# Layer 0 of a four-layer model in one kernel: a batch's end spread over 40 steps, its inverse roots taken on GpSimd

## The chip, the cores and the metric

The kernel runs on one core of a Trainium2 chip, as one program. The metric is the time of one execution on the device in microseconds (us). A difference is read from several runs of both kernels on the same chip.

## The reference

The whole program is four layers, each "normalise, then x + attention(xn) + ffn(xn)", on x of 8 batches x 512 positions x 128 features. The change touches layer 0 alone, whose attention has relative positions (16 heads of 8 features) and ends in a normalisation of its own, and whose feed-forward part is a product with the signs of a weight:

```python
def _layernorm(x, axis=-1, eps=1e-05):
    m = jnp.mean(x, axis=axis, keepdims=True)
    v = jnp.var(x, axis=axis, keepdims=True)
    return (x - m) / jnp.sqrt(v + eps)
...
    scores = scores + (c2p + p2c) / scale          # [8, 16, 512, 512]
    probs = jax.nn.softmax(scores, axis=-1)
    ctx = jnp.einsum('bhqk,bhkd->bhqd', probs, v)
    ctx = jnp.transpose(ctx, (0, 2, 1, 3)).reshape(B, S, H)
    out = ctx @ Wo + bo + hidden_states
    mu = jnp.mean(out, axis=-1, keepdims=True)
    var = jnp.mean(jnp.square(out - mu), axis=-1, keepdims=True)
    out = (out - mu) * jax.lax.rsqrt(var + LN_EPS) * ln_scale + ln_bias
...
    b_weight = jnp.sign(weight)
    return jnp.einsum('bsi,oi->bso', x, b_weight)  # L0 feed-forward
...
    x = x + _L0_attn_ref(xn, ...) + _L0_ffn_ref(xn, L0_ffn_weight)
```

## The kernel before

Layer 0 is one software pipeline over 512 blocks of scores. A block is 128 query positions by 512 key positions of one head; four blocks are a head, 16 heads a batch, so 64 blocks a batch and 8 batches. Each engine runs its own Python loop over the same step number `u`, with `b, r = divmod(u, 64)`: `r` is the step within a batch. The order of the work on each engine is that of its loop, and semaphores tie the engines together.

In step `u` TensorE computes the scores of block `u` (`scores`) and transposes the probabilities of block `u-4` (`p_tr`). VectorE adds the band of relative positions into block `u-1` (`add`, a 192 or 256 column tensor_tensor on PSUM) and takes its negated row maximum (`most`, line 193, once a block). ScalarE takes the exponential of block `u-2` (`exp`, line 167) and copies the transposed probabilities of block `u-5` (`p_out`, line 171). Three PSUM banks hold scores, so the scores of block `v` wait for the exponential of block `v-3`.

Once a head, each in two halves, there are also: a 512 column copy-and-add of the position products by VectorE (`g_out`, at steps with `ib` 1 and 3), a 512 column correction by GpSimd that `g_out` needs (`corr`, at `ib` 0 and 2), and the own band by GpSimd (`own_band`, at `ib` 2: one product of 192 columns and one of 768, which the `add` of the next head needs). GpSimd's order in a head is the second correction, the own band, the first correction of the following head. The band comes back from DRAM by a transfer of SyncE (`write`, `read`). Probabilities times v (`pv`) run on TensorE once per four heads, as four groups of matmuls in steps 5, 7, 9 and 11 of every 16.

All rarer work goes through one PSUM bank, in an order written out by hand: `AHEAD` gives the steps at which the next batch's q, k, far columns, g0 and v are computed, `HEADS` and `ENDS` those at which a finished batch is brought to its end. `small(u)` turns the tables into the list `order`, and each use waits until the one before it has been emptied. The end of batch b-1 runs inside batch b:

- `heads`, `ct`, `mo`: context heads gathered, transposed, multiplied with Wo (plus xn); VectorE adds the bias into `T1` (`tail` 0)
- `sw`: xn times the sign weights; VectorE adds it into X, and takes the mean and variance of `T1` (`tail` 1)
- `root`: ScalarE's square root of the four variances of each partition (line 167)
- `norm`: VectorE's `newton`, that is the reciprocal of the root and one Newton step, and four tensor_scalars of 128 columns that normalise `T1` (`tail` 2)
- `sum`: GpSimd's `tail`, three 512 column tensor_tensors (scale, bias, and the sum into X)
- `last`: VectorE's statistics of X for the next layer's norm (`tail` 3)

The last entry of `ENDS` is for the end of the last batch, which runs in 28 extra steps after the last block, with nothing beside it. After layer 0 every engine waits for all of it (`after_l0`), and layer 1 begins with a norm whose square roots are ScalarE's.

Of the kernel before, what the change touches and what calls it, by code (L numbers as in the profile page):

```python
# [9 lines left out]
ALU = mybir.AluOpType  # L10
# [132 lines left out]
def flat(ap):  # L143
    return ap.rearrange("p a b -> p (a b)")
# [21 lines left out]
def act(ac, out, in_, func, bias=0.0, scale=1.0, accum=None):  # L166
    return ac.e.activation(out, in_, func, bias=bias, scale=scale, accum_out=accum)  # L167
# [12 lines left out]
def tt(en, out, in0, in1, op):  # L180
    return en.e.tensor_tensor(out, in0, in1, op)  # L181
# [24 lines left out]
def newton(dv, y, v, tmp):  # L206

    dv.step(dv.e.reciprocal(y, tmp))
    dv.settle()
    dv.step(tt(dv, tmp, y, y, ALU.mult))  # L210
    dv.settle()
    dv.step(tt(dv, tmp, tmp, v, ALU.mult))
    dv.settle()
    dv.step(ts(dv, tmp, tmp, -0.5, 1.5, ALU.mult, ALU.add))
    dv.settle()
    return tt(dv, y, y, tmp, ALU.mult)


def program(nc, a, out):
    ctx = ExitStack()  # L220
    with ctx:
# [102 lines left out]
        def tr(pe, out, in_):  # L324
# [44 lines left out]
        CTT = flat(T1)  # L369
        nst4 = A0.take(4, 6)  # L370
        lst, lmv, ly, lv, ltmp = A0.take(4, 6), A0.take(4, 2), A0.take(4), A0.take(4), A0.take(4)
        NT0 = dict(st=flat(PB[0].rearrange("p (a b) -> p a b", b=1))[:, 0:192].rearrange("p (a b) -> p a b", b=6),
                   mv=PB[1][:, 0:64].rearrange("p (a b) -> p a b", b=2),
                   y=PB[2][:, 0:32], v=PB[2][:, 64:96], tmp=PB[2][:, 128:160])
# [2 lines left out]

        dv_init, po_init, op_init = sem("dv_init"), sem("po_init"), sem("op_init")
        PT_0, GG_0 = 1, 4
        PGO_0, VA_0 = 1, 3  # L380
        sgn, set_mm, set_dv, set_ac, sel_ok, pg_w, pg_r = (sem("set_" + k) for k in ("sgn", "mm", "dv", "ac", "sel", "pgw", "pgr"))
        s_mm, s_ad, s_mx, s_ex, t_mm, to_a = (sem("l0_" + k) for k in ("s_mm", "s_ad", "s_mx", "s_ex", "t_mm", "to_a"))
        g_mm, g_o, p_cr, p_w = (sem("l0_" + k) for k in ("g_mm", "g_o", "p_cr", "p_w"))
# [12 lines left out]

        AHEAD = {"q": 1, "k": 3, "far": 13, "g0": 15, "v": 35}
        XF_OUT = {2: "q", 4: "k", 14: "far", 16: "g0"}  # L400
        SPLIT_AT = 5
        HEADS = (33, 47, 62)
        ENDS = [{"heads": 17, "ct": 19, "mo": 29, "sw": 31, "root": 34, "norm": 36, "sum": 38, "last": 48}] * NB
        ENDS += [{"heads": 14, "ct": 16, "mo": 18, "sw": 19, "root": 21, "norm": 22, "sum": 23, "last": 25}]

        def small(u):

# [183 lines left out]
        def l0_dv(dv):  # L591
# [100 lines left out]
            def tail(b, k):  # L692
                ps, xs = quarters(PS[:, B_M, :]), slice(b * 4, b * 4 + 4)
                if k == 0:
                    dv.wait_ge(m_mm, number["mo", b, 0] + 1)
                    dv.wait_ge(ld_end, 3 * 16)
                    tt(dv, T1, ps, bc(bot.unsqueeze(1), [128, 4, 128]), ALU.add).then_inc(m_dv, 1)
                elif k == 1:
                    dv.wait_ge(m_mm, number["sw", b, 0] + 1)
                    tt(dv, X[:, xs, :], ps, X[:, xs, :], ALU.add).then_inc(m_dv, 1)  # L700
                    dv.wait_ge(*emptied[number["mo", b, 0]])
                    dv.settle()
                    stats(dv, lmv, lst, T1)
                    dv.settle()
                    ts(dv, lv, lmv[:, :, 1], 1e-7, None, ALU.add).then_inc(tn_v, 1)
                elif k == 2:
                    dv.wait_ge(tn_v, b + 1)
                    dv.wait_ge(tn_q, b + 1)
                    dv.step(newton(dv, ly, lv, ltmp))
                    dv.settle()  # L710
                    for q in range(4):
                        ins = ts(dv, T1[:, q, :], T1[:, q, :], lmv[:, q, 0:1], ly[:, q:q + 1], ALU.subtract, ALU.mult)
                    ins.then_inc(tn_n, 1)
                else:
                    dv.wait_ge(t1_ok, b + 1)
                    stats(dv, NMV[:, xs, :], nst4, X[:, xs, :])
# [5 lines left out]
            for u in range(STEPS0 + 1):  # L722
                n, ib = divmod(u, 4)
                b, r = divmod(u, 64)
                if 0 <= u - 1 < 4 * NBH:
                    add(u - 1)
                if ib in (1, 3) and n + 4 < NBH:
                    g_out(n + 4, ib // 2)
                if 0 <= u - 1 < 4 * NBH:
                    most(u - 1)  # L730
                if b >= 1:
                    at = ENDS[b]
                    if r == at["heads"] + 1:
                        heads_out(b - 1, 3)
                    if r == at["mo"] + 1:
                        tail(b - 1, 0)
                    if r == at["sw"] + 1:
                        tail(b - 1, 1)
                    if r == at["norm"]:
                        tail(b - 1, 2)  # L740
                if b + 1 < NB and r == AHEAD["v"] + 1:
                    v_out(b + 1)
                if b < NB and r - 1 in HEADS:
                    heads_out(b, HEADS.index(r - 1))
                if b >= 1 and r == ENDS[b]["last"]:
                    tail(b - 1, 3)


        def l0_ac(ac):
# [80 lines left out]
            for u in range(STEPS0 + 1):  # L830
                n, ib = divmod(u, 4)
                b, r = divmod(u, 64)
                if 0 <= u - 2 < 4 * NBH:
                    exp(u - 2)
                if 0 <= u - 5 < 4 * NBH:
                    p_out(u - 5)
                if b + 1 < NB:
                    if r in XF_OUT:
                        xf_out(XF_OUT[r], b + 1)
                    k, late = divmod(r - SPLIT_AT, 3)  # L840
                    if 0 <= k < 6 and late == 0:
                        split_ac(b + 1, k // 2, k % 2)
                G, k = divmod(u - 28, 16)
                if k == 0 and 0 <= G < 4 * NB:
                    os_out(G)
                if b >= 1:
                    if r == ENDS[b]["ct"] + 1:
                        ct_out(b - 1)
                    if r == ENDS[b]["root"]:
                        ac.wait_ge(tn_v, b)  # L850
                        act(ac, ltmp, lv, ACT.Sqrt).then_inc(tn_q, 1)


        def l0_po(po):
            po.e.memset(PGO, 0.0).then_inc(po_init, 1)
            for k in range(2):
                po.e.memset(VA[k], 1.0).then_inc(po_init, 1)

            def split(b, k, half):

# [55 lines left out]
            for u in range(STEPS0 + 1):  # L916
                n, ib = divmod(u, 4)
                b, r = divmod(u, 64)
                if ib == 0 and n + 4 < NBH:
                    corr(n + 4, 1)  # L920
                if ib == 2 and n + 1 < NBH:
                    own_band(n + 1)
                if ib == 2 and n + 5 < NBH:
                    corr(n + 5, 0)
                k, late = divmod(r - SPLIT_AT - 2, 3)
                if b + 1 < NB and 0 <= k < 6 and late == 0:
                    split(b + 1, k // 2, k % 2)
                if b >= 1 and r == ENDS[b]["sum"]:
                    tail(b - 1)

# [1642 lines left out]
```

## Time and profile before

| | |
|---|---|
| median of 3 runs | 2280.51 us (2279.85 to 2285.18) |
| profiled execution, its own time | 2277.15 us |
| its span, first to last instruction | 2275.3 us |
| mean granted clock of TensorE | 0.96 |
| busy: TensorE, VectorE, ScalarE, GpSimd | 85%, 78%, 63%, 54% of the span |
| layer 0's blocks, first to last row maximum | 75.4 to 921.3 us |

The profile is one execution recorded by the hardware. A row of a table of stretches gives the stretch, its length, the busy time (and instructions) of PE, PEld, DVE, ACT and POOL in it, the granted clock, the share of the DMA engines and GB/s. "Busy" is the time in which an engine worked on an instruction; issue, branches and waits are not in it. VectorE starts an instruction up to 0.1 us before the one ahead has ended, so what an instruction costs in a row of them is the distance between starts. A row says in brackets how long the engine had sat idle before it, and what ended that. Most helpers record all their calls under one line: 181 is any tensor_tensor, 176 and 177 a tensor_scalar, 157 a matmul. So an instruction is known by its engine, its operation, its shape and its tiles; AR is one large tile that holds most of layer 0's buffers.

### The profile page before, as it was taken

What the parts mean: (1) busy time and instruction counts of PE and PEld (TensorE: products, weight loads), DVE (VectorE), ACT (ScalarE), POOL (GpSimd) and SP (SyncE); (2) the same over time, 40 slices, a digit from 0 to 9 for tenths busy, and PEclk for the clock granted to TensorE, in tenths of its full rate; (3) what the DMA queues carried; (4) which work ended last, traced back from release to release, by engine and by line L of the source; (5) the groups of instructions that cost most, each with busy time, mean ns of one, the idle gap of its engine ahead of it and who ended that gap; (6) DMA issues with size and microseconds to landing.
All of it is one profiled execution on the core that took longest, in us unless ns stands there. A gap on an engine that the chain in (4) does not pass through costs nothing.

```text
span 2275.3 us, 38965 instructions
## 1 busy us (share of the span) xinstructions
PE 1944.4 (85%) x13526; PEld 1473.7 (65%) x13526; DVE 1763.7 (78%) x4099; ACT 1430.5 (63%) x2795; POOL 1223.2 (54%) x1028
## 2 busy tenths in 40 slices
PE   3799898888989898587996999999998468788898
PEld 2566565666666666464683878777876345566797
DVE  7688888888888888457187888888887699873586
ACT  2578777777878777344235666666665257765575
POOL 3777677777777775148053445444543466426400
PEclk9999999999999999789997999999999689999999
DMA  3988788888878786201000000000001000003000
GB/s 105 306 304 303 249 294 274 288 268 278 284 271 281 278 300 227 85 1 35 3 6 1 1 1 1 1 1 1 1 1 31 0 0 1 1 1 98 24 2 38
DMA packets 73877, 264.15 MB, mean 116 GB/s; under 512 B 12273, under 2 KB 32241, under 8 KB 73169
## 3 DMA queue, kind: packets, MB, share of 16 engines
q1 hardware_dynamic: 72304, 254.31, 33.2%
q10 hardware_dynamic: 1376, 7.34, 0.8%
q8 instruction: 109, 1.79, 0.3%
q14 instruction: 88, 0.71, 0.1%
HBM read 140.30 MB, written 121.31 MB: 115 GB/s over the span
## 4 chain that ended last, share of the span: by engine, by line
PE 38%; DVE 8%; ACT 6%; POOL 2%; issue 2%; DMA 0%; POOLq 0%; ACTq 0%; DVEq 0%; SPq 0%
PE PS L157 10%; PE PS L161 7%; PE PS L163 7%; PE PS L162 7%; PE PS L326 7%; ACT AR L167 3%; ACT L167 2%; DVE AR L181 1%; DVE DR L181 1%; DVE PT L181 1%; ACT AR L171 1%; ACT PT L171 1%; DVE AR L185 1%; DVE AR L200 1%; DVE AR L193 1%
## 5 line engine op out<-in xcount | busy, mean ns | idle before, releaser
L167 ACT ACTIVATE AR<-PS,AR 128x512 f32<-128x512 f32 x1008 | 686.6, 688 | 286.8 <-DVE AR L193 178.8
L193 DVE TENSOR_REDUCE AR<-PS 128x1 f32<-128x512 f32 x896 | 616.4, 688 | 119.3 <-PE PS L163 100.5
L326 PE MATMUL PS<-ident,AR 128*128 128x128 f32 x3816 | 584.6, 277 | 86.1 <-ACT AR L171 38.6
L157 PE MATMUL PS<-AR 128*9 128x512 f32 (+8 forms) x4190 | 503.5, 360 | 93.0 <-DVE AR L181 32.9
L326 PEld LDWEIGHTS PS<-ident,AR 128*128 128x128 f32 x3816 | 435.0, 142 | 200.6 <-issue 71.2
L181 POOL TENSOR_TENSOR AR<-AR 128x512 f32<-128x512 f32 (+6 forms) x310 | 380.6, 1244 | 226.9 <-DVE AR L181 97.0
L157 PEld LDWEIGHTS PS<-AR 128*9 128x9 f32 (+5 forms) x4190 | 288.8, 133 | 298.4 <-DVE AR L181 130.1
L171 ACT ACTIVATE AR<-PS 128x512 f32<-128x512 f32 (+3 forms) x612 | 356.4, 587 | 91.8 <-PE PS L326 47.7
L176 POOL TENSOR_SCALAR AR<-AR 128x512 f32<-128x512 f32 x144 | 245.4, 1704 | 293.2 <-DVE AR L1596 219.4
L171 ACT ACTIVATE PT<-PS 128x512 fp32r<-128x512 f32 x320 | 191.5, 599 | 208.3 <-PE PS L326 171.5
L181 DVE TENSOR_TENSOR PS<-PS,AR 128x192 f32<-128x192 f32 (+1 forms) x512 | 201.7, 394 | 118.0 <-PE PS L534 112.0
L181 DVE TENSOR_TENSOR AR<-PS,AR 128x512 f32<-128x512 f32 (+3 forms) x321 | 210.0, 655 | 40.8 <-PE PS L157 36.2
L181 POOL TENSOR_TENSOR AR<-XN,AR 128x192 f32<-128x192 f32 (+1 forms) x170 | 201.5, 1206 | 60.9 <-DMA XN<-scr 42.9
L181 DVE TENSOR_TENSOR PT<-PS,PT 128x512 fp32r<-128x512 f32 x320 | 217.7, 680 | 5.0 <-ACT PT L171 5.0
L181 POOL TENSOR_TENSOR AR<-AR,XN 128x512 f32<-128x512 f32 x144 | 154.3, 1074 | 104.4 <-DVE AR L181 74.8
L534 PE MATMUL PS<-AR 128*128 128x320 bf16 (+3 forms) x1024 | 197.3, 275 | 0.0
L531 PE MATMUL PS<-ident,XN 128*128 128x128 f32 x680 | 131.1, 275 | 0.0
L161 PE MATMUL PS<-MH,XNr 128*128 128x512 f32 x256 | 123.5, 483 | 5.2 <-ACT AR L167 2.8
L176 DVE TENSOR_SCALAR AR<-AR 128x512 f32<-128x512 f32 (+6 forms) x229 | 113.9, 501 | 1.3
L534 PEld LDWEIGHTS PS<-AR 128*128 128x128 bf16 x1024 | 101.1, 99 | 6.2
L163 PE MATMUL PS<-MH,XNr 128*128 128x512 f32 x256 | 102.1, 399 | 0.0
L161 PE MATMUL PS<-PT,VW 128*128 128x512 f32 x256 | 101.5, 396 | 0.0
(157 smaller groups left out, 3001.9 us busy)
## 6 DMA issues: line engine op xcount, KB each, us to landing
scr<-AR SPq DMA_DIRECT2D x128, 800.0 KB, 4.3
XN<-scr SPq DMA_DIRECT2D x85, 768.0 KB, 6.6
AR<-scr SPq DMA_DIRECT2D x43, 768.0 KB, 6.5
AR<-qsc SPq DMA_DIRECT2D x96, 192.0 KB
qsc<-AR SPq DMA_DIRECT2D x96, 128.0 KB, 3.4
AR<-in_wgu SPq DMA_DIRECT2D x16, 256.0 KB, 3.2
X<-in_x ACTq DMA_DIRECT2D x1, 2048.0 KB, 8.5
AR<-in_wi ACTq DMA_DIRECT2D x1, 2048.0 KB, 8.2
```

The lines of the kernel that those rows point to most:

```text
L157: return pe.e.matmul(out, lhsT, rhs, start=start, stop=stop)
L161: pe.e.matmul(out, l[0], r[0], start=start, stop=False)
L162: pe.e.matmul(out, l[1], r[0], start=False, stop=False)
L163: return pe.e.matmul(out, l[0], r[1], start=False, stop=stop)
L167: return ac.e.activation(out, in_, func, bias=bias, scale=scale, accum_out=accum)
L171: return ac.e.activation(out, in_, ACT.Copy, bias=0.0, scale=1.0)
L176: return en.e.tensor_scalar(out, in0, s1, None, op0)
L181: return en.e.tensor_tensor(out, in0, in1, op)
L193: return dv.e.tensor_reduce(out, in_, AX.X, ALU.max, negate=True)
L326: return pe.e.transpose(out, in_, ident[0:k, 0:k])
L531: pe.e.matmul(out, lhsT, rhs, start=start, stop=start, is_transpose=True, skip_group_check=True)
L534: return pe.e.matmul(out, lhsT, rhs, start=False, stop=stop, skip_group_check=True)
```

## The change

The tables of steps are rewritten, the square root on ScalarE becomes a power of -0.5 on GpSimd (four columns, with a constant tile `minus_half`), and the Newton step is written with three instructions in place of five. The X add has a `tail` part of its own. The statistics' `tail` 1 runs at step 32 of VectorE's loop as before, `norm` goes from 36 to 41, the sign-weight matmuls from 31 to 45 and their add from 32 to 46, GpSimd's `tail` from 38 to 47, the last statistics from 48 to 57, and the next batch's v from 35 to 51.

```diff
+def newton3(dv, y, v, tmp):
+
+    dv.step(stt(dv, y, tmp, -0.5, tmp, ALU.mult, ALU.mult))
+    dv.settle()
+    dv.step(tt(dv, y, y, v, ALU.mult))
+    dv.settle()
+    return stt(dv, y, y, 1.5, tmp, ALU.add, ALU.mult)
...
-        AHEAD = {"q": 1, "k": 3, "far": 13, "g0": 15, "v": 35}
+        AHEAD = {"q": 1, "k": 3, "far": 13, "g0": 15, "v": 51}
...
-        ENDS = [{"heads": 17, "ct": 19, "mo": 29, "sw": 31, "root": 34, "norm": 36, "sum": 38, "last": 48}] * NB
-        ENDS += [{"heads": 14, "ct": 16, "mo": 18, "sw": 19, "root": 21, "norm": 22, "sum": 23, "last": 25}]
+        ENDS = [{"heads": 17, "ct": 19, "mo": 29, "stats": 32, "root": 34, "norm": 41, "sw": 45, "sum": 47, "last": 57}] * NB
+        ENDS += [{"heads": 14, "ct": 16, "mo": 18, "stats": 19, "root": 19, "norm": 20, "sw": 19, "sum": 21, "last": 22}]
...
                 elif k == 1:
-                    dv.wait_ge(m_mm, number["sw", b, 0] + 1)
-                    tt(dv, X[:, xs, :], ps, X[:, xs, :], ALU.add).then_inc(m_dv, 1)
                     dv.wait_ge(*emptied[number["mo", b, 0]])
...
-                    dv.step(newton(dv, ly, lv, ltmp))
+                    dv.step(newton3(dv, ly, lv, ltmp))
...
+                elif k == 3:
+                    dv.wait_ge(m_mm, number["sw", b, 0] + 1)
+                    tt(dv, X[:, xs, :], ps, X[:, xs, :], ALU.add).then_inc(m_dv, 1)
...
-                    if r == at["sw"] + 1:
+                    if r == at["stats"]:
                         tail(b - 1, 1)
                     if r == at["norm"]:
                         tail(b - 1, 2)
+                    if r == at["sw"] + 1:
+                        tail(b - 1, 3)
...
-                    if r == ENDS[b]["root"]:
-                        ac.wait_ge(tn_v, b)
-                        act(ac, ltmp, lv, ACT.Sqrt).then_inc(tn_q, 1)
...
+            po.e.memset(minus_half, -0.5).then_inc(po_init, 1)
...
+                if b >= 1 and r == ENDS[b]["root"]:
+                    po.wait_ge(po_init, HALF_0)
+                    po.wait_ge(tn_v, b)
+                    tt(po, ltmp, lv, minus_half, ALU.pow).then_inc(tn_q, 1)
```

## Rows read from the trace of the kernel before

**Rows 1.** The page: busy time and share of each engine.

```profile
PE 1944.4 (85%) x13526; PEld 1473.7 (65%) x13526; DVE 1763.7 (78%) x4099; ACT 1430.5 (63%) x2795; POOL 1223.2 (54%) x1028
```

**Rows 2.** Table of stretches: blocks 28 to 59 of the first and third batch.

```profile
120.89:168.58 47.69, 44.81 (x403) 31.87 (x403) 42.21 (x87) 37.31 (x67) 35.87 (x33) 1.00 0.89 298
327.98:384.85 56.87, 47.81 (x426) 34.25 (x426) 49.37 (x114) 40.18 (x70) 40.26 (x37) 1.00 0.75 251
```

**Rows 3.** Stretches: batch 0's blocks 30, 35, 47; the third's 30, 31, 35, 40-43, 47, 48-51.

```profile
123.48:124.47 0.99, 0.99 (x14) 0.89 (x12) 0.95 (x4) 0.64 (x2) 0.91 (x2) 1.00 0.18 71
...
130.72:132.79 2.07, 2.07 (x23) 1.29 (x20) 2.07 (x4) 1.58 (x3) 1.19 (x2) 1.00 1.00 337
...
148.64:150.60 1.96, 1.56 (x14) 1.06 (x11) 1.93 (x6) 1.96 (x4) 1.96 (x3) 1.00 1.06 336
...
332.36:334.04 1.68, 1.68 (x20) 1.58 (x19) 1.05 (x3) 0.78 (x2) 1.05 (x1) 1.00 0.49 202
334.04:337.51 3.47, 2.19 (x19) 1.61 (x16) 3.40 (x14) 1.57 (x3) 2.37 (x2) 1.00 0.99 328
...
342.27:347.88 5.61, 3.13 (x24) 1.72 (x24) 5.44 (x13) 3.27 (x6) 2.36 (x2) 1.00 1.01 299
...
354.02:360.16 6.14, 6.14 (x56) 3.70 (x50) 5.17 (x12) 4.57 (x9) 6.14 (x7) 1.00 0.68 241
...
363.74:366.87 3.13, 1.65 (x14) 1.06 (x11) 3.06 (x13) 1.96 (x4) 2.54 (x3) 1.00 1.00 313
366.87:371.92 5.05, 3.98 (x37) 3.30 (x38) 4.98 (x11) 3.98 (x8) 3.01 (x4) 1.00 0.76 271
```

**Rows 4.** Timeline, third batch, step 32: VectorE and GpSimd.

```profile
336.55 0.17 DVE L176 TENSOR_SCALAR AR<-AR 128x4 f32<-128x4 f32 x1
...
334.15 2.37 POOL L181 TENSOR_TENSOR AR<-XN,AR 128x192 f32<-128x192 f32 x2 [0.58 <-DVE PS L181]
```

**Rows 5.** Timeline of a later layer: VectorE's small tensor_scalar beside GpSimd.

```profile
1834.06 1.43 DVE L176 TENSOR_SCALAR AR<-AR 128x4 f32<-128x4 f32 x1
...
1831.14 4.33 POOL L181 TENSOR_TENSOR AR<-AR 128x1024 f32<-128x1024 f32 x2
```

**Rows 6.** Timeline, third batch, step 36: VectorE's Newton and normalisation, GpSimd's own band.

```profile
343.08 1.88 DVE L181 TENSOR_TENSOR AR<-AR 128x4 f32<-128x4 f32 x2
...
345.39 1.11 DVE L177 TENSOR_SCALAR AR<-AR 128x128 f32<-128x128 f32 x4
...
342.38 2.36 POOL L181 TENSOR_TENSOR AR<-AR 128x192 f32<-128x192 f32 x2 [0.58 <-DVE PS L181]
```

**Rows 7.** Timeline, GpSimd and VectorE: second batch's steps 56 and 57, batch 0's 40 and 41.

```profile
269.62 2.38 POOL L181 TENSOR_TENSOR AR<-XN,AR 128x192 f32<-128x192 f32 x2
271.95 1.05 POOL L181 TENSOR_TENSOR AR<-AR 128x512 f32<-128x512 f32 x1
...
272.04 0.42 DVE L181 TENSOR_TENSOR PS<-PS,AR 128x256 f32<-128x256 f32 x1
...
138.93 2.37 POOL L181 TENSOR_TENSOR AR<-XN,AR 128x192 f32<-128x192 f32 x2 [2.30 <-DMA XN<-scr]
```

**Rows 8.** Timeline of ScalarE, third batch, around the root.

```profile
339.42 1.28 ACT L167 ACT_TABLE_LOAD   x1
...
342.23 0.69 ACT L167 ACTIVATE AR<-PS,AR 128x512 f32<-128x512 f32 x1
```

**Rows 9.** Timeline of GpSimd, third batch, step 46's correction.

```profile
360.68 1.05 POOL L181 TENSOR_TENSOR AR<-AR,XN 128x512 f32<-128x512 f32 x1
```

**Rows 10.** Timeline, the last batch's end: VectorE; ScalarE, its DMA issue and first root.

```profile
936.27 0.69 DVE L181 TENSOR_TENSOR X<-PS,X 128x512 f32<-128x512 f32 x1 [1.25 <-PE PS L157]
...
939.05 0.18 DVE L208 RECIPROCAL AR<-AR 128x4 f32<-128x4 f32 x1 [0.69 <-ACT AR L167]
...
945.81 0.46 ACTq L1314 DMA_DIRECT2D AR<-in_wo  x1
...
946.85 0.31 ACT L167 ACTIVATE AR<-AR 128x8 f32<-128x8 f32 x2 [8.25 <-DVE AR L176]
```

More of the change, by code:

```diff
@@ L371, in program @@
         lst, lmv, ly, lv, ltmp = A0.take(4, 6), A0.take(4, 2), A0.take(4), A0.take(4), A0.take(4)
+        minus_half = A0.take(4)
         NT0 = dict(st=flat(PB[0].rearrange("p (a b) -> p a b", b=1))[:, 0:192].rearrange("p (a b) -> p a b", b=6),
@@ L379, in program @@
         PT_0, GG_0 = 1, 4
-        PGO_0, VA_0 = 1, 3
+        PGO_0, VA_0, HALF_0 = 1, 3, 4
         sgn, set_mm, set_dv, set_ac, sel_ok, pg_w, pg_r = (sem("set_" + k) for k in ("sgn", "mm", "dv", "ac", "sel", "pgw", "pgr"))
@@ L745, in l0_dv @@
                 if b >= 1 and r == ENDS[b]["last"]:
-                    tail(b - 1, 3)
+                    tail(b - 1, 4)
         def l0_ac(ac):
```

## The prediction

> **What bounds the kernel now.** I read the page first: VectorE is busy 78% and TensorE 85% of the span [rows 1]; a mean over four layers says little, and the diff touches only layer 0. So I cut layer 0 by its own beat. VectorE takes one row maximum (line 193) for each 128x512 block of scores, 64 a batch. "Block k" is the stretch from the start of maximum k of a batch to that of the next; VectorE's extra work of loop step r lies in block r-1. The table of stretches then compares the same blocks of different batches [rows 2]. Batch 0 ends no other batch: its blocks 28 to 59 take 47.69 us. The third batch takes 56.87 us for them, and the second batch's end is what it has more. All 9.2 us between them is that end.
>
> Finer stretches show where [rows 3]. Block 30, before which the sign-weight matmuls now run, takes 1.68 against batch 0's 0.99. Block 31 (line 181's add into X, the statistics, the variance) takes 3.47, VectorE busy 3.40. Block 35 (Newton, four normalisations, the v copy) takes 5.61 against 2.07, VectorE busy 5.44: nothing but VectorE decides there, and TensorE is busy only 3.13. Blocks 40 to 43 take 6.14 with TensorE busy all of it and VectorE only 5.17, since the four probability-times-v groups run there; the like four blocks without them (48 to 51) take 5.05, VectorE busy 4.98. So there are two regimes. VectorE sets 12 to 19, 28 to 35, 44 to 51 and 60 to 3; TensorE sets the others, and there VectorE has 6.14 - 5.05 = 1.09 us of slack in four blocks. A VectorE instruction costs its issue interval in the first kind and nothing, up to the slack, in the second.
>
> **The change, term by term**, for one of the seven batch ends inside the loop, against the third batch.
>
> 1. *Sign-weight matmuls leave step 31.* They had waited there for the T1 add. Block 30 falls to batch 0's 0.99 [rows 3]: **-0.69**. They come back at step 45, in a region that VectorE sets, behind the same kind of queue: I take the same 0.69 there, **+0.69** (nothing at best, twice that at worst).
>
> 2. *The add into X leaves step 32.* It takes 0.60 from its start to the next one's, so block 31 would be 2.87. But the variance's tensor_scalar now comes 0.6 sooner after the maximum. Now it starts at 336.55, at the very end of GpSimd's two own-band products (334.15 to 336.52) [rows 4]. Elsewhere the same 4-column instruction beside a GpSimd tensor_tensor takes 1.43 us and not 0.17, and ends with GpSimd's [rows 5]. I expect it to be held to the same moment: -0.60 + 0.56 = **-0.04** (-0.6 if it is not held). The add returns at step 46 in a VectorE region: **+0.60**.
>
> 3. *Newton and the normalisations leave step 36.* Block 35 falls from 5.61 to batch 0's 2.07 [rows 3]: **-3.54**. What goes: five Newton steps, of which the first tensor_tensor is held for some 1.7 us by GpSimd's 128x768 product (1.88 for the pair of it and an ordinary one), and four tensor_scalars [rows 6]. The v matmuls and v copy leave steps 35 and 36 too, but come back at 51 and 52, the same place of the 16-step pattern: I count zero for both together.
>
> 4. *Newton at step 41.* Three instructions at some 0.20 from start to start, as the small ones of [rows 6]: 0.60. Four normalisations, 1.03 (the 1.11 of their row less the 0.08 by which the next instruction starts early). And a hold: all three Newton instructions read two SBUF operands. Where block 40's neighbour sixteen steps on is undisturbed, GpSimd ends its own-band pair at 272.0 and starts the next 1.05 us correction at 271.95; VectorE is free at 272.04 [rows 7]. So it meets the correction, not the long own-band product: 271.95 + 1.05 - 272.07 = 0.93 us held. The ends are 0 (the instruction slips in first) and some 2.6: in batch 0 the own band, late from its read, runs from 138.93 to 141.30 while VectorE is free at 139.52 [rows 7], 1.75 us, and the correction behind it could hold the second instruction for another 0.85. 0.93 is the row nearest. From 0.60 + 1.03 + 0.93 = 2.56 the slack of blocks 41 and 43 is taken, 1.09: **+1.47**.
>
>    The Trainium skill ("SBUF — State Buffer", Who interferes with whom) says that the pair of ports which VectorE shares with GpSimd is an exclusive lock, taken by a VectorE instruction with two SBUF inputs against a GpSimd one that reads SBUF. By that rule step 41 is no safe place either; the held row above agrees, with 1.88 us for two 4-column instructions, and the 0.93 above is what it comes to. Without such a rule the term would be 0.54.
>
> 5. *X's statistics go from step 48 to 57.* Out of a VectorE region: block 47 takes 3.13 against batch 0's 1.96, **-1.17**. In block 56, where TensorE sets again, the same 1.17 meets the same slack of 1.09: **+0.08**.
>
> 6. *The root moves from ScalarE to GpSimd.* ScalarE loses two table loads of 1.28 us and a 0.20 us root [rows 8]. I count **zero**: during them VectorE and TensorE go on, and the exponential behind them starts at 342.23 just when VectorE enters its 5.6 us block, in which it catches up. If that cover were gone, they would cost 2.8. The Trainium skill ("ScalarE: Activation LUTs", What ACT_TABLE_LOAD costs) gives 2.66 us for a switch with its drain, 5.3 for both; by it alone the removal would be the larger part of the change. The trace shows 2.81 from the first load's start to the next exponential's, and no other engine waiting for it.
>    GpSimd gets the power after the correction of step 34, where it then sits idle some 2 us for VectorE. No row shows a power. Below it is bounded by what four columns take on VectorE, 0.17 us [rows 6], above by GpSimd's own-band pair, 2.36 us for 960 columns; I take 1.0, since four columns are few and a power is not one operation. Behind it queue the correction of step 36, the own band (2.36) and a correction, due at step 41. From that correction's end to step 41 pass some 11.5 us in batch 0, 4.5 of them GpSimd's own work, so some 7 us are free and all of the range costs nothing.
>
> 7. *GpSimd's three 512-column products move from step 38 to 47*, 3.9 us. Behind them wait the correction for step 51 and the own band for step 53. In the third batch the correction ahead of them starts at 360.68 [rows 9]: 360.68 + 1.05 + 3.9 + 1.05 = 366.7 for the next, which VectorE uses at 368.87, and 2.36 more, 369.0, for the own band, used after 371.9. Both are some 2 us ahead: **zero**.
>
> Sum: -0.69 + 0.69 - 0.04 + 0.60 - 3.54 + 1.47 - 1.17 + 0.08 = **-2.60 us** a batch end, times seven **-18.2 us**.
>
> *The last batch's end* is a bare chain [rows 10]. Statistics no longer wait for the sign matmuls, 1.25, and the add, 0.60: -1.85. The root's hop is 0.69, its own 0.20 in it; by GpSimd I take 0.25 + 1.0, so +0.56. Two Newton steps fewer, -0.40. But ScalarE's last table load, hidden now in a wait, must come before layer 1's first root, behind the barrier and two DMA issues: they end at 946.27, plus 1.28 is 947.55 and not 946.85, +0.70. Together **-1.0**.
>
> The profiled execution took 2277.15 (span 2275.3), 0.15% under the median of 2280.51. It goes to 2277.15 - 19.2 = 2258.0; as a median of runs, 2280.51 - 19.2 = **2261.3 us**, 0.8% faster.
>
> **Rivals.**
> *A, the hold comes in full and the slack isn't there.* Own-band reads land late without the old stall, as in batch 0, so Newton is held 2.6 us, and TensorE gives back nothing: +1.67 + 1.09 leaves +0.16 a batch, nothing in all: 2280.6, no change. For it: the DMA engines are busier where there is no stall (0.89 of batch 0's stretch against 0.75 [rows 2]). Against: at the undisturbed place the own band starts 0.2 us after the add that it waits for, its read long there [rows 7]. Chance 0.13.
> *B, no hold at all.* Newton meets no GpSimd instruction, and the variance neither: -0.93 - 0.56 a batch, -10.4: 2250.9. Chance 0.15.
> *C, GpSimd becomes late (slower).* The power stands in a queue that is busy 4.5 of every 5.05 to 6.1 us (two corrections and an own band). It costs nothing up to some 7 us and a microsecond each beyond. To lose 0.3% it must use up 19.2 + 6.8 in seven batches, 3.7 us each: a power of about 11 us, 2.7 us a column, where a column of the own band costs 2.5 ns (2.36 us over 960). At 12 us it gives back 5 a batch: 2261.3 + 35 = 2296. Against: nothing on GpSimd in this trace is near it; for: a power is not an ordinary operation, and no row prices it. Chance 0.06.
> *D, the table loads were on the path*: 2.8 more a batch, 2241.7. Against: VectorE is busy 5.44 of 5.61 behind them. Chance 0.06.
> The forecast itself 0.60, its own range 2254 to 2269 (the ends of terms 1, 2 and 4, a microsecond a batch either way).
>
> **How the numbers follow.** 0.3%, 6.8 us, is about what a measurement tells from no change. Faster: 0.60 + 0.15 + 0.06 and a fifth of A, 0.84; same 0.10; slower 0.06. Eight in ten: from B, with its neighbours' microsecond, 2248, to halfway to A, 2272.
>
> **What would show it.** Block 35 near 1.5 to 2.1; block 30 near 1.0; block 31 unchanged near 3.4, its variance held; a Newton instruction of 0.9 to 1.1 us in block 40, block 40 about 3.6 and the blocks 41 to 43 shorter by about 1; block 47 near 2; block 56 longer by 1.2 with 57 to 59 shorter; no table loads between exponentials; the power well under 2 us. I am wrong if the own band or a correction of steps 41 to 55 makes VectorE wait for GpSimd, or if the blocks that TensorE sets grow by what VectorE was given.

## The result, and the profile after

The changed kernel takes 2260.2 us (median of 4 runs, 2258.81 to 2263.45) beside 2280.18 us for the kernel before on the same chip (4 runs, 2279.63 to 2285.18): a ratio of 0.991, 95% interval 0.9892 to 0.9927. The forecast was 2261.3. Its profiled execution took 2258.81, span 2257.0, 18.3 less than the span before. The page's line of busy times hardly differs from [rows 1]; means over the program say nothing here either.

```profile
PE 1943.3 (86%) x13526; PEld 1476.4 (65%) x13526; DVE 1760.9 (78%) x4083; ACT 1409.8 (62%) x2773; POOL 1230.6 (55%) x1037
```

The table of stretches of the kernel after, for the blocks of [rows 2] and [rows 3]. Columns: start:end and length; busy time (and instructions) of PE, PEld, VectorE, ScalarE, GpSimd; granted clock, DMA share, GB/s. First blocks 28 to 59 of batch 0 and of the third batch, then the third batch's 30, 31, 35, 36 to 39, 40, 41 to 43, 47 and 56 to 59.

```profile
120.44:167.51 47.07, 44.82 (x403) 31.85 (x403) 42.24 (x87) 37.14 (x67) 36.01 (x34) 1.00 0.90 302
323.14:376.30 53.16, 46.95 (x421) 33.84 (x421) 48.60 (x112) 36.88 (x66) 41.16 (x38) 1.00 0.78 267
327.52:328.51 0.99, 0.76 (x9) 0.79 (x10) 0.96 (x3) 0.27 (x1) 0.82 (x1) 1.00 0.13 52
328.51:331.86 3.35, 2.04 (x17) 1.45 (x15) 3.28 (x13) 1.97 (x4) 2.54 (x3) 1.00 1.04 353
...
335.92:337.39 1.47, 0.94 (x9) 0.65 (x8) 1.47 (x3) 1.47 (x4) 1.47 (x3) 1.00 1.11 374
337.39:344.13 6.74, 6.74 (x66) 4.15 (x67) 5.21 (x12) 5.10 (x10) 4.91 (x5) 1.00 1.00 302
344.13:347.64 3.51, 3.51 (x37) 2.02 (x36) 3.37 (x11) 1.18 (x2) 1.56 (x2) 1.00 0.75 295
347.64:351.63 3.99, 2.89 (x31) 2.26 (x23) 3.96 (x8) 2.91 (x6) 2.29 (x3) 1.00 0.44 154
...
356.26:358.22 1.96, 1.76 (x15) 1.18 (x12) 1.92 (x5) 1.89 (x4) 1.88 (x3) 1.00 1.05 359
...
370.07:376.30 6.23, 5.79 (x53) 3.48 (x53) 6.13 (x19) 4.09 (x8) 4.26 (x5) 1.00 0.67 247
```

What a batch's end costs over batch 0 went from 9.2 us to 53.16 - 47.07 = 6.1. Block 35, 5.61 before, is now 1.47. Block 40 is the new long one, 3.51. In blocks 40 to 43 VectorE is busy 3.37 + 3.96 = 7.33 of the 7.50 us and TensorE only 6.40: with Newton in it, VectorE sets this stretch too.

The timeline of VectorE and GpSimd in the third batch, kernel after: the variance of step 32, the power of step 34 (the second of the pair at 332.02, 1.03 us; the first is a correction, 1.01), Newton and the normalisations of step 41.

```profile
330.43 0.65 DVE L176 TENSOR_SCALAR AR<-AR 128x4 f32<-128x4 f32 x1
...
344.73 0.99 DVE L185 SCALAR_TENSOR_TENSOR AR<-AR 128x4 f32<-128x4 f32 x1
345.75 0.16 DVE L181 TENSOR_TENSOR AR<-AR 128x4 f32<-128x4 f32 x1
...
346.15 1.12 DVE L177 TENSOR_SCALAR AR<-AR 128x128 f32<-128x128 f32 x4
...
329.24 1.81 POOL L181 TENSOR_TENSOR AR<-XN,AR 128x768 f32<-128x768 f32 x1
332.02 2.04 POOL L181 TENSOR_TENSOR AR<-AR 128x512 f32<-128x512 f32 x2 [0.96 <-DVE AR L181]
...
342.31 2.38 POOL L181 TENSOR_TENSOR AR<-XN,AR 128x192 f32<-128x192 f32 x2
344.64 1.06 POOL L181 TENSOR_TENSOR AR<-AR 128x512 f32<-128x512 f32 x1
```

The rows show two holds, that is, VectorE instructions drawn out until a GpSimd one ends. The variance's 4-column instruction takes 0.65 us and not 0.17, and ends at 331.08, GpSimd's 128x768 product at 331.05. Newton's first instruction starts at 344.73, just behind the start of a correction that runs to 345.70, and ends at 345.72; the next two, alone, take 0.16. The root is no visible part of this: VectorE doesn't wait for the power anywhere inside a batch.

### The profile page after: what moved, and what is told of

It reads as the page before. It is cut to its first block, busy times and chain, and to the rows that moved or that the text cites. A ratio compares the mean times of both kernels' runs of the same rounds, so it can differ in the third digit from the quotient of the medians.

```text
span 2257.0 us, 38937 instructions
## 1 busy us (share of the span) xinstructions
PE 1943.3 (86%) x13526; PEld 1476.4 (65%) x13526; DVE 1760.9 (78%) x4083; ACT 1409.8 (62%) x2773; POOL 1230.6 (55%) x1037
## 4 chain that ended last, share of the span: by engine, by line
PE 38%; DVE 9%; ACT 5%; POOL 2%; issue 2%; DMA 0%; POOLq 0%; ACTq 0%; DVEq 0%; SPq 0%
PE PS L157 9%; PE PS L161 7%; PE PS L163 7%; PE PS L162 7%; PE PS L335 7%; ACT AR L167 2%; DVE AR L181 2%; ACT L167 1%; DVE PT L181 1%; DVE DR L181 1%; ACT AR L171 1%; DVE AR L185 1%; DVE AR L193 1%; DVE AR L200 1%; DVE XN L177 1%
## 5 line engine op out<-in xcount | busy, mean ns | idle before, releaser
L181 POOL TENSOR_TENSOR AR<-AR 128x512 f32<-128x512 f32 (+6 forms) x318 | 388.3, 1238 | 248.7 <-DVE AR L181 89.0
```

## Experiments

Each run is set beside runs of the kernel before that were measured together with it (medians 2278.04, 2280.37 and 2278.43). Undoing one part of the change is measured from the kernel after, whose ratio is 0.991. The diffs show the lines or words that differ, without what stands around them.

**1. The new steps with ScalarE's root.** Only the steps are changed; the power is gone, root and table loads are back on ScalarE, and Newton has its five instructions.

```diff
-    tt(po, ltmp, lv, minus_half, ALU.pow).then_inc(tn_q, 1)
+    act(ac, ltmp, lv, ACT.Sqrt).then_inc(tn_q, 1)
-                    dv.step(newton3(dv, ly, lv, ltmp))
+                    dv.step(newton(dv, ly, lv, ltmp))
```

> The changed kernel's steps, but the root is ScalarE's square root again and Newton has its five instructions. Two ideas of what the power on GpSimd is worth. (a) The table loads are hidden wherever they stand: only two more Newton instructions, 0.2 us each, in seven batches, some 3 us: 2263 us, block 34 to 35 at 1.0 and 1.5 us as in the changed kernel. (b) They were hidden before only by VectorE's long block 35 behind them; at the new steps that cover is gone and most of the 2.8 us of two loads and a root shows in each of seven batches: 2260 + 3 + up to 19.6, so 2275 to 2282, with VectorE idle in blocks 34 to 36 waiting for TensorE, which waits for ScalarE. The prediction's words were: if that cover were gone, they would cost 2.8.

Measured: 2279.28 us (10 runs), ratio 0.9997, 0.9986 to 1.0008. The whole gain is gone. Timeline of the third batch of this kernel, ScalarE, then VectorE and TensorE:

```profile
336.37 1.28 ACT L167 ACT_TABLE_LOAD   x1
...
339.19 0.69 ACT L167 ACTIVATE AR<-PS,AR 128x512 f32<-128x512 f32 x1
...
342.42 0.37 DVE L181 TENSOR_TENSOR PS<-PS,AR 128x192 f32<-128x192 f32 x1 [3.19 <-PE PS L544]
...
340.41 1.12 PE L335 MATMUL PS<-ident,AR 128*128 128x128 f32 x4 [2.33 <-ACT AR L171]
```

And its table of stretches: blocks 35 and 36 to 39 of the third batch, then block 35 of the fourth:

```profile
338.54:343.29 4.75, 2.88 (x14) 2.68 (x15) 1.56 (x3) 4.04 (x7) 2.52 (x3) 0.60 1.00 343
343.29:351.30 8.01, 8.01 (x64) 4.33 (x65) 5.26 (x11) 4.58 (x8) 3.87 (x4) 0.81 0.54 141
448.63:452.51 3.88, 2.00 (x16) 1.60 (x16) 1.56 (x4) 3.87 (x7) 2.58 (x3) 1.00 0.99 326
```

VectorE is idle for 3.19 us in block 35, behind TensorE, which has itself waited 2.33 us for a ScalarE copy that came behind the loads. In this batch there is a second cost: the granted clock is 0.60 over block 35, and the four transposes at 340.41 take 1.12 us, against 0.66 for the like four at 374.26 of the kernel after. Blocks 34 to 39 take 4.57 us more than in the kernel after, which is more than the 2.8 us from the first load to the next exponential. In the fourth batch TensorE waits the same 2.33 us and the clock stays at 1.00: block 35 takes 3.88 and not 4.75, and the whole batch is 2.15 us longer than that of the kernel after, the two more Newton instructions (0.19) among them. The other six batches have the low clock. Over all seven this trace is 22.7 us longer, 3.2 a batch. So with the move the table loads lie on the path, at about 2 us in the batch where the clock stays up and more where it falls.

**2. The old steps with GpSimd's power** and Newton's three instructions: the other half of the change.

```diff
-    act(ac, ltmp, lv, ACT.Sqrt).then_inc(tn_q, 1)
+    tt(po, ltmp, lv, minus_half, ALU.pow).then_inc(tn_q, 1)
-                    dv.step(newton(dv, ly, lv, ltmp))
+                    dv.step(newton3(dv, ly, lv, ltmp))
```

> The kernel before with its own steps, but the root is GpSimd's power and Newton has three instructions. (a) As the prediction has it, the loads cost nothing at the old steps: the gain is two Newton instructions, 0.4 us in seven batches, 3 us, and the last batch's end is shorter by 0.4 and longer by the power's hop and the late table load, about +0.9: 2278 us, block 35 near 5.2 us. (b) If the loads were on the path at the old steps, 2.8 a batch more: 2258 us. The hold in block 35 stays in both, near 1.7 us.

Measured: 2281.07 us (10 runs), ratio 1.0004, 0.9994 to 1.0015. No change. Block 35 falls only from 5.61 to 5.23, the two Newton instructions fewer. Timeline of this kernel's third batch, VectorE, then TensorE:

```profile
338.96 1.70 DVE L181 TENSOR_TENSOR AR<-AR 128x4 f32<-128x4 f32 x1
...
343.53 0.40 PE L157 MATMUL PS<-AR 128*128 128x128 bf16 x4 [2.85 <-DVE AR L181]
...
345.33 1.12 PE L335 MATMUL PS<-ident,AR 128*128 128x128 f32 x4 [0.52 <-ACT AR L171]
```

The own band holds Newton for 1.70 us as before. Even the 0.39 saved isn't kept: blocks 36 to 39 take 7.58 (granted clock 0.77) and not 6.14, and such a stretch of low clock stands at this place in each of the second to seventh batches. TensorE in the kernel before, timeline of the same place in the third batch, and one row of the second:

```profile
343.46 0.66 PE L326 MATMUL PS<-ident,AR 128*128 128x128 f32 x4 [1.40 <-ACT AR L171]
...
348.02 0.40 PE L157 MATMUL PS<-AR 128*128 128x128 bf16 x4 [1.43 <-DVE AR L181]
...
241.00 1.08 PE L326 MATMUL PS<-ident,AR 128*128 128x128 f32 x4 [0.53 <-ACT AR L171]
```

There TensorE waits in two pieces, 1.40 us for ScalarE, which is late by its table loads, and 1.43 for VectorE. Without the loads it waits once, 2.85. In the kernel before the clock stayed at 1.00 here in the third to seventh batches, but in the second, with the same two waits, it fell to 0.50 for 3.4 us and four transposes took 1.08. That one long wait instead of two brings the clock down is therefore likely and not shown.

With the table loads out of the way the step itself, VectorE's 5.2 us, is what it was. Taking both runs together, neither half does anything alone (+0.0% each), and the two make 0.9%; in run 2 the low clock is part of the reason.

**3. Newton and the normalisations one step later, 42.**

```diff
-"root": 34, "norm": 41, "sw": 45
+"root": 34, "norm": 42, "sw": 45
```

> The changed kernel with Newton and the normalisations at step 42 in place of 41. (a) If the 0.98 us by which Newton's first instruction is drawn out is the correction that GpSimd runs at that moment, one step later it has ended: Newton's instructions take 0.16 us each in five of seven batches, and where the own band came late (second and fifth batch, 2.4 us held) about 1 us stays: 0.98 x 5 + 1.4 x 2 = 7.7 us less, about 2252.5. (b) If the first instruction is long for another reason (its wait for the power's semaphore, a first use of its form), it stays at 0.98 us and the time at 2260. (c) If the slack that TensorE gives is lost one step later, the gain is smaller by up to 0.5 us a batch, 2256.

Measured: 2247.91 us (4 runs), ratio 0.9864, 0.9844 to 0.9885: 0.5% better than the kernel after. In five of the seven batches Newton's first instruction takes 0.15 us, with no GpSimd product beside it. In the second and third it is still held; the third, on the timeline of VectorE and GpSimd:

```profile
343.17 0.36 DVE L185 SCALAR_TENSOR_TENSOR AR<-AR 128x4 f32<-128x4 f32 x1
343.57 0.97 DVE L181 TENSOR_TENSOR AR<-AR 128x4 f32<-128x4 f32 x1
...
341.14 2.38 POOL L181 TENSOR_TENSOR AR<-XN,AR 128x192 f32<-128x192 f32 x2 [1.43 <-DMA XN<-scr]
343.47 1.05 POOL L181 TENSOR_TENSOR AR<-AR 128x512 f32<-128x512 f32 x1
```

There the own band waited 1.43 us for its read, so its end and the correction came as late as Newton. The third batch takes 104.65 us against 104.02 in the kernel after, with 3.4 us at half clock in blocks 33 to 35 that the kernel after doesn't have there; the fifth takes 104.01 against 107.16. The hold was real, and worth most where the own band was late. Of the 11.3 us by which this span is shorter than that of the kernel after, 7.9 lie in the seven batches; the rest lies in parts of the program that the edit doesn't touch.

**4. The v copy back at its old place.**

```diff
-        AHEAD = {"q": 1, "k": 3, "far": 13, "g0": 15, "v": 51}
+        AHEAD = {"q": 1, "k": 3, "far": 13, "g0": 15, "v": 35}
```

> The changed kernel with the next batch's v matmuls at step 35, as before, and not 51. (a) The prediction counted the move as worth nothing: 2260. (b) The blocks of the two kernels say otherwise: blocks 34 to 39 lose 0.69 + 0 where v leaves, blocks 50 to 55 grow by 0.07 where it comes, so in eight batches the move back costs up to 0.6 each, 4 to 5 us: 2264 to 2265.

Measured: 2261.19 us (4 runs), ratio 0.992, 0.9901 to 0.9939: no difference from 0.991 that can be measured. Its third batch is 104.47 against 104.02, 0.45 more. The seven together are 3.2 us longer in its trace, but four of them have a stretch of low clock and in the kernel after only two, so the traces don't price the move either.

**5. X's statistics back at step 48.**

```diff
-"sum": 47, "last": 57}
+"sum": 47, "last": 48}
```

> The changed kernel with X's statistics at step 48 again, not 57. (a) The prediction priced this move at -1.17 + 0.08 a batch: undone it costs 1.09 in seven batches, 7.6 us: 2268. (b) The changed kernel's blocks show 0.49 paid back in block 61, where ScalarE comes late: undone it costs 1.17 - 1.17 + 1.14 - 0.52 = 0.6 a batch, 4.3 us: 2264 to 2265. (c) If GpSimd's sum, now only a step ahead, is what the statistics wait for at step 48, 3 to 4 us a batch more: above 2280. The sum starts at step 47 and takes 3.9 us, so (c) is the likeliest to spoil the reading; then block 47 is above 5 us.

Measured: 2266.2 us (4 runs), ratio 0.9945, 0.9928 to 0.9961, between the two. Block 47 takes 3.47 and not 1.96. In the timeline of VectorE the statistics also wait for GpSimd's sum, which ends only a step before:

```profile
358.70 0.87 DVE L200 BATCH_NORM_STATS2 AR<-X 128x6 f32<-128x128 f32 x4 [0.25 <-POOL X L181]
```

Over 64 blocks the third batch pays 105.37 - 104.02 = 1.35 us. 1.51 go in block 47, and block 61 gives back 0.48: with the statistics at 57 it takes 2.02 instead of 1.54. VectorE waits 0.39 us for TensorE there, and ScalarE works from 375.62 to 379.43 without a pause; that ScalarE's copies are what makes TensorE late is likely and not shown. (0.44 of the 1.35 lie in blocks 0 to 29, where nothing was moved.)

**6. Four more powers** behind each other, into four columns that nothing reads, ahead of the one that is used.

```diff
+                    for _ in range(4):
+                        po.settle()
+                        po.step(tt(po, minus_half2, lv, minus_half, ALU.pow))
                     tt(po, ltmp, lv, minus_half, ALU.pow).then_inc(tn_q, 1)
```

> The changed kernel with four more powers of the same size ahead of the one used, into a tile that nobody reads: GpSimd's root takes 5.2 us and not 1.03. (a) The prediction: some 7 us are free before step 41, so this costs nothing: 2260. (b) If the queue behind it is tight (correction of step 36, own band, correction), VectorE waits for GpSimd in blocks 38 to 40 and each batch loses 1 to 4 us: 2267 to 2288.

**7. Twelve more**: the same with range(12).

> The changed kernel with twelve more powers: GpSimd's root takes 13.4 us. (a) The prediction's rival C: free up to some 7 us and a microsecond each beyond: 13.4 - 7 = 6.4 us in seven batches, 45 us: about 2305. (b) If GpSimd catches up in the stall or the free part is larger, less: 2285. (c) If GpSimd is never late, 2260.

Measured: five powers (5.2 us) 2273.5 us (2265.6 to 2277.07, 10 runs), ratio 0.9964, 0.9949 to 0.9979; thirteen (13.4 us) 2336.21 (4 runs), ratio 1.0255, 1.0239 to 1.027. Both pay their extra length once in the bare chain of the last batch (VectorE's wait for the power is 5.43 us there with five, 1.20 with one). Inside a batch, third batch of each, timeline of VectorE and GpSimd with five powers:

```profile
343.93 1.28 DVE L185 SCALAR_TENSOR_TENSOR AR<-AR 128x4 f32<-128x4 f32 x1
345.25 0.97 DVE L181 TENSOR_TENSOR AR<-AR 128x4 f32<-128x4 f32 x1
...
342.80 2.39 POOL L181 TENSOR_TENSOR AR<-XN,AR 128x192 f32<-128x192 f32 x2
```

and with thirteen, VectorE and TensorE:

```profile
357.23 0.69 DVE L181 TENSOR_TENSOR AR<-PS,AR 128x512 f32<-128x512 f32 x1 [7.45 <-POOL AR L181]
...
357.98 0.61 PE L157 MATMUL PS<-AR 128*128 128x128 bf16 x4 [6.82 <-DVE AR L181]
```

With five, VectorE waits for no GpSimd result in the batch; the own band starts only 0.5 us ahead of block 40 (343.33) and not 1.8 (342.31 ahead of 344.13 in the kernel after), so Newton now meets its last product and the correction behind it, and block 40 is 4.61 and not 3.51. With thirteen the first result due is the correction that `g_out` of step 39 adds, not Newton's at 41: VectorE waits 7.45 us for it, and the batch is 9.6 us longer than in the kernel after. From five to thirteen powers, 8.2 us more of them, the third batch grows by 113.62 - 105.11 = 8.5. The profiled execution with five powers took 2266.75, among its shortest, so about 7 us of the median have no place in this trace.

**8. Statistics at step 37, root at 38, Newton at 42.** What run 3 gained and the two regimes together suggest this: the statistics go where TensorE sets the pace. Run 3 is in it, so what the statistics' move is worth is read against run 3.

```diff
-"mo": 29, "stats": 32, "root": 34, "norm": 41
+"mo": 29, "stats": 37, "root": 38, "norm": 42
```

> A new version: the changed kernel with T1's statistics at step 37 and not 32, the power at step 38, Newton at 42. (a) If two regimes are the right reading, the statistics (1.88 us from block 31's 3.35 to 1.47) leave blocks that VectorE sets for blocks 36 to 39 that TensorE sets; these took 6.73 in the changed kernel against 5.05 where VectorE sets, so 1.68 of the 1.88 vanishes: 1.7 a batch, 12 us below the version with Newton at 42 alone (2247.9): 2236. (b) If what TensorE gives back is paid again by ScalarE, as in block 61, half of it: 2242. (c) If they meet GpSimd's products or bring Newton into its correction again: 2248 or more.

Measured: **2238.69 us** (2237.16 to 2242.98, 4 runs), ratio 0.983, 0.9812 to 0.9848, the best here, 9.2 us below run 3; the two intervals just overlap, and the seven batches of its trace are 9.7 us shorter than run 3's. Its table of stretches, third batch, blocks 31, 35, 36 to 39 and 40 to 43:

```profile
323.49:324.96 1.47, 1.46 (x14) 1.16 (x13) 1.47 (x3) 1.47 (x4) 1.47 (x3) 1.00 1.00 401
329.06:330.53 1.47, 0.95 (x9) 0.66 (x8) 1.47 (x4) 1.47 (x4) 1.01 (x3) 1.00 1.12 380
330.53:337.50 6.97, 6.49 (x59) 3.87 (x58) 6.83 (x20) 4.58 (x10) 5.91 (x6) 1.00 0.95 296
337.50:344.46 6.96, 6.93 (x65) 4.64 (x64) 6.79 (x18) 4.59 (x10) 4.39 (x5) 1.00 0.69 236
```

Block 31 gives back 3.35 - 1.47 = 1.88 us, in every batch, and blocks 36 to 39 take 0.23 more: the same nine instructions (eight of the statistics, and the variance's) are paid for in the one and nearly free in the other. In the other six batches blocks 36 to 39 take 6.73 to 7.15, but 7.92 in the fourth, where GpSimd holds the variance's instruction for 1.65 us. The third batch is 102.05 us against 104.02.

**9. The variance's instruction on GpSimd too**, in the kernel of run 8. The text put down before the run speaks of a Newton step without the 1e-7. The kernel that was run leaves nothing out: GpSimd adds the 1e-7, and Newton reads the sum.

```diff
-                    ts(dv, lv, lmv[:, :, 1], 1e-7, None, ALU.add).then_inc(tn_v, 1)
+                    po.step(ts(po, lv, lmv[:, :, 1], 1e-7, None, ALU.add))
+                    po.settle()
                     tt(po, ltmp, lv, minus_half, ALU.pow).then_inc(tn_q, 1)
```

> The version with statistics at 37 and Newton at 42, whose tensor_scalar that adds 1e-7 to the variance is moved from VectorE to GpSimd, ahead of the power; Newton multiplies with the variance itself, without the 1e-7. (a) VectorE no longer meets the lock there: in that version it took 0.27 to 1.65 us where 0.17 is usual, so 0.4 to 1.5 us a batch go, less what the slack hid anyway: 2233 to 2237. (b) All of it lies in slack: 2238. (c) GpSimd's extra instruction, about 0.3 us, delays the correction of step 39 or the own band, and Newton is held longer: 2241.

Measured: 2242.01 us (4 runs), ratio 0.9844, 0.9817 to 0.9871, no difference from run 8. VectorE is rid of a held instruction (0.70 us in run 8) and block 36 falls from 2.98 to 2.23, but blocks 36 to 39 together go from 6.97 only to 6.73, with TensorE busy all of them. VectorE's time there isn't what they wait for, the fourth batch apart, where they go from 7.92 to 6.73. Timeline of GpSimd: the added instruction, then the power and a correction.

```profile
334.37 0.23 POOL L176 TENSOR_SCALAR AR<-AR 128x4 f32<-128x4 f32 x1
334.68 2.07 POOL L181 TENSOR_TENSOR AR<-AR 128x4 f32<-128x4 f32 x2
```

**10. ScalarE's root in the kernel of run 8**, with Newton's five instructions: run 1 again, but in a stretch that TensorE sets. The diff is run 1's.

> The version with statistics at 37 and Newton at 42, but ScalarE's square root at step 38 with its two table loads, and five Newton instructions. (a) The loads cost what ScalarE's queue can't hide wherever no long VectorE block stands behind them: as at step 34 of the changed kernel's steps, about 3 us a batch and low granted clock after it, 2238.7 + 20 = 2259 or more. (b) Where TensorE sets the pace ScalarE has slack too (4.6 busy of 6.14), and here Newton and the normalisations come only four steps later, so about 1.5 us a batch is hidden: 2250. (c) Hidden in full: 2242.

Measured: 2244.05 us (4 runs), ratio 0.9848, 0.9824 to 0.9872: not told apart from run 8, where the same root made up the whole 20 us between run 1 and the kernel after. Timeline, third batch, ScalarE and VectorE:

```profile
335.19 1.28 ACT L167 ACT_TABLE_LOAD   x1
...
338.01 0.69 ACT L167 ACTIVATE AR<-PS,AR 128x512 f32<-128x512 f32 x1
...
340.37 0.37 DVE L181 TENSOR_TENSOR PS<-PS,AR 128x192 f32<-128x192 f32 x1 [0.89 <-PE PS L544]
```

The lag is the same 2.8 us, but VectorE waits 0.89 and not 3.19, and the granted clock stays 1.00; the third batch takes 102.88 against 102.05. Over the seven batches this trace is 5.7 us longer than run 8's, 0.8 a batch with the two more Newton instructions in it: small, not nothing.

## Why the prediction was right, and which of its sizes were not

Term by term, third batch, from the starts of the row maxima in both traces.

| term | predicted | measured | where it is read |
|---|---|---|---|
| 1, sign matmuls leave 31 | -0.69 | -0.69 | block 30, 1.68 to 0.99 |
| 1, they return at 45 | +0.69 | +0.45 | blocks 44 and 46 |
| 2, variance, add leaves | -0.04 | -0.12 | block 31, 3.47 to 3.35 |
| 2, add returns | +0.60 | +0.59 | block 45, 1.54 to 2.13 |
| 3, Newton leaves 36 | -3.54 | -3.54 | block 35 to batch 0's old 2.07 |
| 3, v matmuls and copy | 0 | -0.63 | blocks 34 to 39 and 50 to 55 |
| 4, Newton at 41 | +1.47 | +1.36 | blocks 40 to 43, 6.14 to 7.50 |
| 5, statistics to 57 | -1.09 | -0.65 | blocks 47, 56 to 59, 61 |
| sum | -2.60 | -3.20 | batch, 107.22 to 104.02 (the rows add up to -3.23: rounding, and block 60) |

**Right, with its mechanism.** Term 4 rested on a correction meeting Newton for 0.93 us: five of the seven batches show 0.96 to 0.99 for that instruction, less 0.16 of its own. (The prediction's sum has 272.07 where it names 272.04, which would make 0.96 of its 0.93.) Run 3 moves it by one step and the hold goes, in five batches of seven, with 10 us of the time, 8 of them in the traces' seven batches. The variance was held to GpSimd's end as term 2 said. The Trainium skill ("SBUF — State Buffer", Who interferes with whom), which has the shared port pair as an exclusive lock for VectorE's instructions with two SBUF inputs, agrees with those 0.99 us; the tensor_scalar held for 0.65 has one such input only, and the Trainium skill lists that kind among those that can ask for the pair as well. Term 3's size, the regimes of [rows 3] and block 56's return of the statistics (+1.17 in 56, -1.14 in 57 to 59) came as forecast.

**Right on its condition.** Term 6 was counted at zero, and the text named the cover, VectorE's 5.6 us block, and the price if it were gone, 2.8. Runs 1 and 2 show both. In the kernel before the loads cost nothing, since taking them away alone (run 2) gives nothing and block 35 loses only the two Newton instructions. One reading of the prediction was not right there: it saw no other engine waiting for the loads, but TensorE waits 1.40 us for ScalarE's copy behind them in block 35. VectorE doesn't wait, and it sets that block. The move takes the cover away, and with the loads still there it gives nothing either (run 1). So rival D, by which the loads were on the path before, is out, though the two halves can't be priced apart: the 20 us belong to their being made together. The Trainium skill ("ScalarE: Activation LUTs", What ACT_TABLE_LOAD costs) gives 2.66 us a switch with its drain. The rows show 1.28 for a load and 2.82 from the first load to the next exponential, and no drain of that size; what the pair costs, nothing in the kernel before, about 2 us in run 1's batch at full clock and at most 0.8 a batch in run 10, was set by what lay beside it.

**Mis-sized.** *The v copy*, counted at zero because it comes back at the same place of the 16-step pattern. In the old place it also stood in front of TensorE's stretch: blocks 34 and 35 lose 0.69 and 0.60, and 36 to 39 regain 0.59. That is read from blocks; run 4 finds no difference in the whole time, so only the argument of zero by pattern fell, not the total. In run 4's third batch Newton comes later against GpSimd and is held less (0.64 us and not 0.99), which gives 0.36 back. *Term 5's return* had a second part that was not seen, block 61 (+0.48, run 5). *The sign matmuls' return* was 0.24 too dear. *The free time on GpSimd*, "some 7 us": run 6 uses 4.1 of it and pays 1.10 us in block 40. The count asked when a result is due and not when the product moves onto VectorE's own two-operand instruction; and the first result due is the correction that `g_out` of step 39 adds, two steps sooner than assumed (run 7). The power itself, 1.03 us, was the 1.0 taken, so rival C had no chance to act. Run 7 bears out its slope, a microsecond for a microsecond, but not its start: thirteen powers are 12.4 us more than one and VectorE waits 7.45, so by an estimate from these two some 5 us more than the one power were free, a root of 6 us and not of 7. The batch pays 9.6 and not 7.45 because Newton is held longer (block 40 takes 5.13 and not 3.51) and the clock is at 0.50 behind the wait.

**The last batch's end**, timeline of the kernel after, VectorE, GpSimd and ScalarE:

```profile
918.44 0.17 DVE L176 TENSOR_SCALAR AR<-AR 128x4 f32<-128x4 f32 x1
919.81 0.16 DVE L185 SCALAR_TENSOR_TENSOR AR<-AR 128x4 f32<-128x4 f32 x1 [1.20 <-POOL AR L181]
...
918.69 1.02 POOL L181 TENSOR_TENSOR AR<-AR 128x4 f32<-128x4 f32 x1 [25.96 <-DVE AR L176]
...
926.95 1.28 ACT L167 ACT_TABLE_LOAD   x1 [14.10 <-issue]
```

The hop over GpSimd is 919.81 - 918.61 = 1.20, with 1.25 forecast. From the T1 add to X's sum the chain is 1.72 shorter (1.69 forecast), and the table load that is no longer hidden adds 1.04 (0.70 forecast). That is -0.7 where -1.0 was said; and the T1 add itself comes 14.4 us after the last maximum, not 13.0, with 3.4 us of half clock from 913.3 in between. So the end as a whole lost 0.7 instead of gaining 1.0.

**The total agrees better than its parts.** The third batch gained 3.20 where 2.60 was forecast, but the seven gained 18.3, which is 2.61 each. (Batch 0, which had been counted at nothing, took 1.7 less as well, 97.05 and not 98.74; but run 2, whose batch 0 has the steps of the kernel before, takes 96.94 for it, so that isn't the change's doing. The first maximum comes 0.6 later, the end lost 0.7, and the layers behind it differ by 0.3, which makes the span's 18.3.) The fifth gained only 0.16. On the timeline of VectorE, TensorE and GpSimd, and in the table of stretches of that place:

```profile
554.20 1.70 DVE L185 SCALAR_TENSOR_TENSOR AR<-AR 128x4 f32<-128x4 f32 x1
555.93 0.97 DVE L181 TENSOR_TENSOR AR<-AR 128x4 f32<-128x4 f32 x1
...
560.30 0.40 PE L157 MATMUL PS<-AR 128*128 128x128 bf16 x4 [2.62 <-DVE AR L181]
...
553.51 3.38 POOL L181 TENSOR_TENSOR AR<-AR 128x192 f32<-128x192 f32 x3 [1.69 <-DMA AR<-scr]
```

```profile
561.70:565.10 3.40, 3.40 (x20) 3.21 (x20) 1.73 (x5) 2.83 (x6) 3.40 (x4) 0.50 0.99 316
```

Here the own band's read came late and held Newton twice, as rival A had it from batch 0 (1.75 and 0.85 there, 1.54 and 0.81 here); TensorE was idle for 2.62 us, and 1.4 us later came 3.4 us at half clock. Rival A's hold came in two batches of seven, not in all; the second, the other one, gained 3.77 us all the same, among other things because the kernel before had its own stretch of low clock there (blocks 36 to 39 took 7.76 and not 6.14). So which batches the clock falls in moves single batches by more than most terms. What the terms missed in each direction came out even; that is luck and not a finding. Why the read is late in these batches and not in the others wasn't tried.

## What to carry to other kernels

Before moving a small piece of work, find for each stretch which engine sets its length, by comparing the same stretch with and without the extra work: nine small instructions cost 1.88 us in a stretch that VectorE sets and 0.23 in the third batch (0 to 0.4 in most) in one that TensorE sets. A cost that is hidden is hidden by a particular stall, so removing the stall makes it due; change the two together, and test each half alone before crediting either. Place VectorE's short instructions with SBUF operands by GpSimd's schedule: one loop step was worth 8 to 10 us here.

## What the runs showed of the hardware that was not expected

The granted clock of TensorE can make a stall dearer than its length. Around waits of TensorE of 2.33 us (run 1), 2.85 (run 2), 2.62 (fifth batch after) and 6.82 us (run 7), the granted clock went to 0.50, the 1.2 GHz level, for 3.4 or 6.8 us; four transposes went from 0.61 to 1.12 us. In run 2 that took more than the 0.39 us that had been saved. But the length of the last wait doesn't tell when it happens. The clock stayed at 1.00 behind waits of 2.33 us (run 1, fourth batch), 2.32 (second batch after) and 2.19 to 2.72 (run 6, all seven batches). And it fell for 3.4 us behind waits of 1.43 us (second batch before) and 1.44 (sixth batch after). What decides it stays open here.

A power of 128x4 in fp32 took 1.01 to 1.03 us on GpSimd, about as long as its 128x512 product (1.05), while a 128x4 tensor_scalar took 0.23 there (run 9). So it is the power that is dear, and not an instruction of four columns as such; no run has a power of another width.
